# Five engine orders laid out anew, and a second group of states kept in PSUM and multiplied by c on VectorE

## The reference, cut to what matters

```python
x = x + ssm(layernorm(x)); x = x + ffn(layernorm(x))
# ssm: 256 hidden channels, 16 states each
u, o = x @ W_in.T                       # halves
u = silu(causal_conv4(u) + conv_b)
delta_lo, b, c = u @ W_gate.T           # 64, 16, 16 columns
delta = softplus(delta_lo @ W_delta.T + delta_bias)
h = exp(A * delta[..., None]) * h + (delta * u)[..., None] * b      # scan over positions
y = einsum(h, c) + D * u
out = (y * sigmoid(o) * o) @ W_out.T
# ffn: 8 experts of width 176, the best 2 of 8 by softmax, weights renormalised and scaled by 2.5,
#      and a shared expert of width 352: silu(x @ w_gate) * (x @ w_up) @ w_down
```

## Time and profile before

| | us |
|---|---|
| median of 3 runs (lowest, highest) | 1346.92 (1346.78, 1347.88) |
| profiled execution, its own time | 1347.99 |
| its span, first to last instruction | 1346.3 |
| PE busy, matmuls / weight loads | 1160.7 / 930.5 |
| POOL busy | 1142.5 (85%) |
| DVE busy | 1126.5 (84%) |
| ACT busy | 1044.9 (78%) |

### The profile page before, as it was taken

One profiled execution on the slowest core, in us unless ns is written; L12 is line 12 of the kernel. 1 busy time (PEld: TensorE's weight loads), 2 busy tenths in 40 slices (PEclk: granted clock), 3 DMA queues, 4 the chain that ended last, 5 costly groups with the idle time before them and its releaser, 6 DMA issues. The chain is left out here.

```text
span 1346.3 us, 26240 instructions
## 1 busy us (share of the span) xinstructions
PE 1160.7 (86%) x9075; PEld 930.5 (69%) x9075; DVE 1126.5 (84%) x1762; ACT 1044.9 (78%) x2155; POOL 1142.5 (85%) x536
## 2 busy tenths in 40 slices
PE   3455999999999989999999999999999999998787
PEld 2323777777777777777777777777777777776677
DVE  3466799999998999899988989989889998898853
ACT  3877788888888788888887888888888888887742
POOL 3299799999999999999999999999999999999820
PEclk8767899999999999999999999999999999998899
DMA  4343323434343224443332333333432334333000
GB/s 109 108 101 88 85 72 86 100 100 104 73 103 97 74 77 100 103 100 81 95 103 70 79 99 100 100 87 90 103 81 74 93 100 100 91 78 98 5 5 9
DMA packets 71486, 115.09 MB, mean 85 GB/s; under 512 B 8173, under 2 KB 30394, under 8 KB 71354
## 3 DMA queue, kind: packets, MB, share of 16 engines
q1 hardware_dynamic: 67178, 110.71, 32.4%
q10 hardware_dynamic: 4176, 2.70, 0.7%
HBM read 41.04 MB, written 5.24 MB: 34 GB/s over the span
## 5 line engine op out<-in xcount | busy, mean ns | idle before, releaser
L405 POOL TENSOR_TENSOR inject<-rep,bc 128x1024 f32<-128x1024 f32 x256 | 604.1, 2384 | 10.7 <-DMA rep<-dd 9.9
L414 POOL TENSOR_TENSOR read<-state,bc 128x1024 f32<-128x1024 f32 x224 | 529.1, 2377 | 35.7 <-DVE state L689 28.1
L689 DVE TENSOR_TENSOR_SCAN state<-decay_ps,inject 128x1024 f32<-128x1024 f32 x224 | 508.3, 2281 | 27.7 <-ACT decay_ps L483 25.3
L483 ACT ACTIVATE decay_ps<-rep,neg_a 128x255 f32<-128x255 f32 x1024 | 423.1, 460 | 27.1 <-DVE state L689 24.8
L923 PE MATMUL work_ps<-xn2T_part,ffn_gate 128*128 128x256 f32 x1344 | 218.7, 300 | 46.2 <-ACT g_silu L471 39.4
L471 ACT ACTIVATE g_silu<-work_ps 128x512 f32<-128x512 f32 x224 | 134.5, 601 | 133.1 <-PE work_ps L923 111.6
L923 PEld LDWEIGHTS work_ps<-xn2T_part,ffn_gate 128*128 128x128 f32 x1344 | 182.0, 195 | 77.8 <-ACT g_silu L471 55.0
L957 PE MATMUL acc_ps<-ffn_down,features 128*128 128x128 f32 (+1 forms) x1792 | 229.0, 277 | 0.0
L957 PEld LDWEIGHTS acc_ps<-ffn_down,features 128*128 128x128 f32 (+1 forms) x1792 | 213.0, 191 | 4.5
L707 DVE TENSOR_TENSOR features<-g_silu,work_ps 128x512 f32<-128x512 f32 x224 | 152.2, 680 | 75.2 <-ACT g_silu L471 40.1
L932 PE MATMUL work_ps<-xn2T_part,ffn_up 128*128 128x256 f32 x1344 | 197.6, 287 | 0.0
(11 more groups left out here) (138 smaller groups left out, 1394.4 us busy)
## 6 DMA issues: line engine op xcount, KB each, us to landing
rep<-dd SPq DMA_DIRECT2D x256, 256.0 KB, 4.7
bc<-bc_rows SPq DMA_DIRECT2D x64, 512.0 KB, 4.8
x_in<-in_L_attn_x_dram SPq DMA_DIRECT2D x32, 128.0 KB, 2.1
out_dram<-result SPq DMA_DIRECT2D x32, 128.0 KB, 1.8
bc_rows<-g_sb SPq DMA_DIRECT2D x32, 32.0 KB
state<-in_L_ffn_w_gate_dram ACTq DMA_DIRECT2D x1, 704.0 KB, 4.4
read<-in_L_ffn_w_up_dram ACTq DMA_DIRECT2D x1, 704.0 KB, 5.9
ffn_down<-in_L_ffn_w_down_dram ACTq DMA_DIRECT2D x1, 704.0 KB, 6.9
```

Source lines behind the costliest of these rows:

```text
L405: pool.tensor_tensor(inject[:, at % RI], du_all, b_all, ALU.mult).then_inc(inject_done, 1)
L414: pool.tensor_tensor(read[:, at % RR], state[:, at % RS], c_all, ALU.mult).then_inc(read_done, 1)
L483: last = act.activation(decay_ps[:, at % 2, j, 1:T], rep[(HALVES * n + half) % RP][:, j, 0, 1:T], ACT.Exp, scale=neg_a[:, col:col + 1])
L689: dve.tensor_tensor_scan(to, decays, inject[:, at % RI].rearrange("p j t -> p (j t)"), 0.0, ALU.mult, ALU.add).then_inc(state_done, 1)
```

## The change

`OWN` becomes a pair of groups, 0 and 4. Group 0's scan too writes back into `decay_ps`, DVE multiplies it by c, and POOL has 6 reads a sequence. `read_own_group(0)` stands behind `scan(0)`, three products, the x statistics and a `take_y`, and `read_own_group(4)` one product behind `scan(4)`. The decays of group 2 now wait for `decay_zero` like those of group 6. There is still one `read_own` tile. The semaphore counts follow.

The orders of DVE, ACT, PE and POOL within a step are laid out anew. The order in which waits are written changes too, so that another one of them is held by the instruction, and some that an earlier wait of the same engine covers are left out. SP's order stays.

```diff
-OWN = 4
-OTHERS = GROUPS - 1
+OWN = (0, 4)
+OTHERS = GROUPS - len(OWN)
...
 def inject_group(n, q):
-                    pool.wait_ge(rep_in[half], 16 * JB * (n + 1))
-                    pool.wait_ge(b_in, 16 * (n + 1))
+                    if g == 0:
+                        pool.wait_ge(rep_in[half], 16 * JB * (n + 1))
+                        if half == 0:
+                            pool.wait_ge(b_in, 16 * (n + 1))
                     pool.wait_ge(state_done, count(at - RI + 1))
 def read_group(n, q):
-                    pool.wait_ge(c_in, 16 * (n + 1))
                     pool.wait_ge(state_done, GROUPS * n + q + 1)
+                    if q == 0:
+                        pool.wait_ge(c_in, 16 * (n + 1))
...
                 injects(3)
-                reads(0)
                 reads(1)
+                reads(2)
                 injects(4)
-                reads(2)
                 reads(3)
...
 def decays(n, q):
-                    act.wait_ge(rep_in[half], 16 * JB * (n + 1))
-                    if q == OWN + 2:
-                        act.wait_ge(decay_zero, n + 2)
+                    if g == 0:
+                        act.wait_ge(rep_in[half], 16 * JB * (n + 1))
+                    if (q - 2) % GROUPS in OWN:
+                        act.wait_ge(decay_zero, owned_before(at - 1) + 1)
...
-                if on(1) and not on(0):
-                    act.wait_ge(ffn_loaded, 16 * len(ffn_loads))
-                    act.wait_ge(padded, 2)
-                    act.copy(ffn_gate[0][:], gate_staged).then_inc(ffn_high, 1)
-                    act.copy(ffn_up[0][:], up_staged).then_inc(ffn_high, 1)
...
 scan(q)
-                    if q == OWN:
+                    if q in OWN:
                         to = decays
...
-                def read_own_group():
+                def read_own_group(q):
+                    at = own(k, q)
+                    dve.wait_ge(state_done, GROUPS * k + q + 1)
                     dve.wait_ge(c_in, 16 * (k + 1))
-                    dve.wait_ge(state_done, GROUPS * k + OWN + 1)
-                    dve.wait_ge(sum_done, count(GROUPS * (k - 1) + OWN + 1))
+                    if at >= 1:
+                        dve.wait_ge(sum_done, GROUPS * ((at - 1) // len(OWN)) + OWN[(at - 1) % len(OWN)] + 1)
-                    dve.tensor_tensor(read_own[:], decay_ps[:, OWN % 2], c_all, ALU.mult).then_inc(read_own_done, 1)
+                    dve.tensor_tensor(read_own[:], decay_ps[:, q % 2], c_all, ALU.mult).then_inc(read_own_done, 1)
...
 def gated_up(p):
+                    dve.wait_ge(ffu_mm, at + 1)
                     dve.wait_ge(silu_done, at + 1)
-                    dve.wait_ge(ffu_mm, at + 1)
```

More of the change, by code:

```diff
@@ L59, in others, with own, owned_before @@
 def others(n, q):
-    return OTHERS * n + (q if q < OWN else q - 1)
+    return OTHERS * n + q - sum(o < q for o in OWN)
 def of_others(at):
-    n, q = divmod(at, OTHERS)
-    return GROUPS * n + (q if q < OWN else q + 1)
+    n, i = divmod(at, OTHERS)
+    return GROUPS * n + [q for q in range(GROUPS) if q not in OWN][i]
+def own(n, q):
+    return len(OWN) * n + OWN.index(q)
+def owned_before(at):
+    n, q = divmod(at, GROUPS)
+    return len(OWN) * n + sum(o < q for o in OWN)
 def comb_chunks(i):
@@ L490, in body @@
                     silu(0)
+                    silu(1)
                 if on(2):
@@ L574, in body @@
                     silu(5)
+                if on(1) and not on(0):
+                    act.wait_ge(ffn_loaded, 16 * len(ffn_loads))
+                    act.wait_ge(padded, 2)
+                    act.copy(ffn_gate[0][:], gate_staged).then_inc(ffn_high, 1)
+                    act.copy(ffn_up[0][:], up_staged).then_inc(ffn_high, 1)
+                if on(3) or on(-1):
+                    act.activation(neg_mean[:], mean_var[:, :, 0], ACT.Copy, scale=-1.0).then_inc(ln_small, 1)
                 if on(2):
@@ L726, in pairs @@
                             gated_up(p)
+                if on(0):
+                    scan(0)
+                pairs(0)
                 if on(3):
@@ L964, in body @@
                     gates(1, f)
-                    pe.wait_ge(silu_done, pair(0))
-                    ups(1, f)
                 if on(-1):
@@ L969, in body @@
                 if on(-2):
+                    pe.wait_ge(silu_done, pair(0))
+                    ups(1, f)
                     pe.wait_ge(h_done, pair(0))
@@ L986, in body @@
                     last.then_inc(gate_mm, 1)
-                if on(-2):
-                    pe.wait_ge(silu_done, pair(2))
-                    ups(3, f)
                 if on(-3):
@@ L993, in body @@
                         down(chunk, f - 1)
+                if on(-2):
+                    pe.wait_ge(silu_done, pair(2))
+                    ups(3, f)
+                if on(2):
+                    n = k + 2
+                    if on(1):
+                        pe.wait_ge(gate_done, k + 2)
+                    pe.wait_ge(ln1_done, n + 1)
+                    for j in range(TILES):
+                        last = pe.matmul(xnT_ps[:, j * P:(j + 1) * P], xn[:, j, :], ident[:], start=(j == 0), stop=False,
+                                         skip_group_check=True)
+                    last.then_inc(xnT_mm, 1)
                 if on(-1):
@@ L1022, in body @@
                               skip_group_check=True).then_inc(xnT_rest, 1)
-                if on(-2):
+                if on(0):
+                    pe.wait_ge(result_done, count(k - 2))
+                    pe.wait_ge(y_taken, HALVES * k)
+                    sum_states(k, 0)
+                    sum_states(k, 1)
+                if on(-2):
+                    if on(-1):
+                        pe.wait_ge(x1_done, k)
+                    else:
+                        pe.wait_ge(silu_done, pair(3))
+                    gates(4, f)
                     pe.wait_ge(comb_split, 2 * f + 2)
@@ L1075, in body @@
                     ups(6, f)
+                    pe.wait_ge(silu_done, pair(6))
+                    spread_comb(0)
                 if on(0):
```

180 lines of the change are left out of this document (80 added, 100 removed).

## The result

The changed kernel takes 1282.28 us in the median of four runs (1280.32 to 1282.99), beside 1346.99 (1346.78 to 1347.88) for the kernel before: a ratio of 0.952, 95% interval 0.950 to 0.953. It is 64.7 us faster. I had forecast 1312 and a range of 1296 to 1333. The direction was right.

A forecast was written before the change was run, and what follows sets the result against it. The prediction took a loop through DVE, ACT and PE as the bound, no engine being full. 28 steps at 37.2 instead of 38.27 us gain 30, start and end 5: 35 us, so 1312 us, range 1296 to 1333.

The forecast's parts named there:

- The loop: Steady step: DVE's half, PE's half, 0.1 for two hand-overs, 0.3 wait on ACT, 0.2 unlisted hand-overs: 37.2 us against 38.27.
- DVE's half: On DVE from the product of pair 2 to the split router weights (comb_parts): 9.7 us a step.
- PE's half: On PE from the transposes of comb_parts through conv, down, xn2T and router to ups(2): 26.9 us a step.
- PE has transposes, a sum and conv before gates(5) ... and waits 0.3: On PE, 3.85 us of work before gates(5), silu(4) ready at 4.1: a wait of 0.3 us a step.
- I add 0.2 for hand-overs I did not write down: Allowance on the steady loop for hand-overs between engines not listed: 0.2 us a step.
- I take 0: Cost of separate waits on the loop's stalled instructions: taken as 0, bounds 0 and 7 us.
- The start: Steps -1 to 2: ACT's later FFN weight copies credited 2 us, POOL's dropped read credited 2.
- The end: Last steps: combT comes after the Ln table load, 1.28 us once, credited as 1.
- Rival 1: Shorter loop; DVE's load alone sets the step at about 36.5 us: 1292 us, chance 0.12.
- Rival 2: Unseen new waits come up because DVE has no room, 37.9 us a step: 1333 us, chance 0.13.
- Rival 3: ACT's decays of group 2 come late for scan(2), ways tie at 5.4 and 5.45: 1354 us, chance 0.09.
- Rival 4: The old loop stays at 38.2 us a step, only start and end gain: 1342 to 1345, chance 0.06.

The follow-up runs named there:

- a2_old_waits: The changed kernel with the waits in their old order and number, timed beside a1_again: 1291.83 us.
- a1_again: The changed kernel itself, unchanged, timed again on the same chip as a2_old_waits: 1283.91 us.
- e1_own_only: The kernel before, old orders and waits, with only group 0 kept in PSUM and read by DVE instead of POOL: 1389.85 us, ratio 1.031.
- e2_orders_only: The changed kernel with group 0's read given back to POOL, so the new orders and waits alone: 1291.62 us, ratio 0.958.
- e5_z_less_late: The changed kernel with DVE's z_less moved back behind scan(6) and a weighing: 1327.69 us, ratio 0.985.
- e6_own0_late: The changed kernel with DVE's own read of group 0 moved behind scan(1): 1299.24 us, ratio 0.964.
- g4_old_act_dve: e2_orders_only with the old orders and waits of ACT and DVE, PE's order kept new: 1586.07 us, ratio 1.178.
- g1_old_scalar: e2_orders_only with ACT's old order and waits, those of DVE and PE kept new: 1720.17 us, ratio 1.278.
- g3_old_tensor: e2_orders_only with PE's old order and waits, those of ACT and DVE kept new: 1497.12 us, ratio 1.112.

## Why the prediction was right or wrong

**The loop** was named rightly, and both halves hold, as shown above. Its length was forecast as 37.2 and is 36.3. The 0.9 of difference by terms:

- DVE's half: 9.63 for 9.7, 0.07.
- PE's half: 26.57 for 26.9, 0.33. PE is busy all but 0.1 of it. Here the step that failed is "of PE's 35.16 us, outside this half lies ... busy 7.76": I took PE's busy time as a fixed amount of work. In the changed kernel the same matmuls are busy 34.31 a step.
- "PE has transposes, a sum and conv before gates(5) ... and waits 0.3": PE reaches gates(5) at 654.57, 4.12 after the transposes start, but it doesn't wait there: its own work ahead of them took 4.12 where the old rows gave 3.85, that time is part of the 26.57, and silu(4) was ready at 4.07. 0.3 too much.
- "I add 0.2 for hand-overs I did not write down": there were none. 0.2 too much.

Over 28 steps these four make 25 us (55.1 for 30.0). Of the 66.1 us between the spans, where 35 were forecast, that leaves 8 of the start and -2 of the end.

**Waits at the instructions.** "I take 0" with the argument that three injects in a row lose nothing. That row is of waits long met, and some on the loop are not: a2_old_waits took 7.9 us more than a1_again, at least 2.4 of it in the steady part and so inside the 0.9 above. It was above the value and, as a whole, just above the bound of 7.

**The start.** Credited 4 and measured 12.0. The copies were right (1.8 at the first inject). What failed is "POOL's read counts there once, 2.4": steps 0 and 1 are set by POOL, so it counts in each of them (2.8 and 2.95), and step 2 brought 4.45. The runs with half of the change tell the two apart. e1_own_only, with PE's old order, shortens the first three intervals by 3.2, 3.3 and 0.8, and e2_orders_only, with seven reads, by 0.5, 0.55 and 4.9. So steps 0 and 1 are the own group's, and step 2 is mostly the orders'. There, before, PE waits ahead of the sum of group 5, with the transposes for xn2T queued behind it; the timeline of PE in the kernel before:

```profile
129.72 1.08 PE L915 MATMUL acc_ps<-read,sum_sel 128*32 128x256 f32 x8 [8.08 <-POOL read L414]
```

In the changed kernel the sum stands behind, and PE waits only for ACT's xn; its timeline:

```profile
119.26 1.20 PE L1144 MATMUL work_ps<-ident,xn 128*128 128x128 f32 x4 [5.10 <-ACT xn L626]
```

The granted clock in that interval also rose, from 0.76 to 0.86, and no run separates what the clock gave from what the order gave. **The end** was credited with 1 and lost 1.0; why stays open.

**Rival 1** (DVE's load alone, 36.5 a step) has the nearest time, 1292, by a wrong cause: e5_z_less_late and e6_own0_late leave DVE's load as it is and lose 1.5 and 0.47 a step. "DVE has to hold 36.0. That is the new floor" was wrong as well: DVE is busy 35.08. **Rival 2** (new waits at 37.9) did not come. **Rival 3** is a tie, as computed, and e6_own0_late shows its price. The load of a table lasts 1.28 and decays(2) start 1.29 after its start (643.12, 644.41), much as in the kernel before, and not the 2.66 us of the Trainium skill's page "ScalarE: Activation LUTs", section "What ACT_TABLE_LOAD costs". **Rival 4** falls.

The range failed because every allowance on the loop (0.1, 0.3, 0.2) was made in one direction. Rival 1 stood for a shorter loop, but it had only 0.12, and the range left out its lower half. That its 1292 lies nearest is luck: its 36.5 a step was worked out from a DVE load of 36.0, which measured 35.08.

## What to carry to other kernels

Where no engine is full and each waits for another once a step, as here, take the orders of all engines as one thing: compute the loop that a new set gives, and don't price the moves one by one. One engine's old order among new ones cost 7 to 15 us a step here, clock included, where the whole set gained 1.9. Take the length of each stretch of the loop from rows where that stretch ran without stalls. A read taken off the busiest engine was worth 0.1 us a step here after the orders were right, and cost 1.6 before. Before a step that is longer than its neighbours is explained by waits, look at the granted clock in it.

## What the runs showed of the hardware that was not expected

Busy time was not a fixed sum. Both kernels have 9075 matmuls, and PE is busy 35.16 us a step before and 34.31 after, at a granted clock of 1.00 in both. DVE, with the new work that I priced at 1.29 us, went from 34.71 to 35.08. In e1_own_only, with that same work in the old orders, it is busy 36.01 in a step at full clock (358.02 to 397.51), just the 36.0 of the prediction, and in e2_orders_only, with the old work in the new orders, 34.14. So the order is worth 0.6 to 0.9 us of busy time on each of the two engines, and a floor worked out from the old busy share was that much too high. One reading is that where an engine stalls, the tail of its last instruction is not covered by the next; no run isolated it. More idle time alone doesn't do it: in a step of 44.72 us of g4_old_act_dve, PE is busy 35.27 and DVE 34.90.

The granted clock of PE is 1.00 in 300:900 of both kernels, and in 400:1000 it is 0.84 in g1_old_scalar and 0.93 in g3_old_tensor, where PE is busy 489.1 and 517.0 us of the 600. So a part of what these two lose is the clock.
